# Relative-position stage by pairs of heads, with the first head's maxima inside it

## The reference

```python
qkv = x @ qkv_w + qkv_b                       # x: layer-normed, S = 2304 tokens, 12 heads of 32
attn = einsum('bqd,bkd->bqk', q * scale, k)
rel_h = einsum('bhwc,hkc->bhwk', qr, Rh)      # Rh[y, k] = rel_pos_h[y - k + 47]
rel_w = einsum('bhwc,wkc->bhwk', qr, Rw)
bias = (rel_h[..., :, None] + rel_w[..., None, :]).reshape(B * nh, S, S)
out = softmax(attn + bias) @ v
x = x + out @ proj_w + proj_b                 # then x + experts(layernorm(x)), two of eight by gates
```

## Time and profile before

| | us |
|---|---|
| median of 3 runs (lowest, highest) | 2328.25 (2328.11, 2330.27) |
| the profiled execution, its own time | 2332.33 |
| its span | 2330.6 |
| TensorE busy | 2061.9 (88%) |
| VectorE busy | 1783.8 (77%) |
| ScalarE busy | 1661.2 (71%) |
| GpSimd busy | 756.0 (32%) |

### The profile page before, as it was taken

How to read it: one execution, slowest core, us unless ns; L and a number is a source line. 1 busy time by engine, 2 the same in 40 slices (tenths; PEclk the granted TensorE clock), 3 DMA queues, 4 the chain that set the end, 5 groups by cost and what they waited for, 6 DMA issues and landing times. The chain is left out here.

```text
span 2330.6 us, 38125 instructions
## 1 busy us (share of the span) xinstructions
PE 2061.9 (88%) x12356; PEld 1882.0 (81%) x12356; DVE 1783.8 (77%) x3335; ACT 1661.2 (71%) x2909; POOL 756.0 (32%) x523
## 2 busy tenths in 40 slices
PE   6933347999999999999999999965799999999997
PEld 6922226888888888888888888744799999999997
DVE  5654446999999999999999998556677777777774
ACT  3344405888888888888888888912577778877785
POOL 0030031445444554445454445530122211221121
PEclk9955577999999999999999999977799999999999
DMA  6778893465544655546555454132566766777774
GB/s 208 223 164 188 189 168 72 85 127 101 105 95 77 125 106 101 103 76 116 107 101 113 78 106 79 57 122 93 170 212 215 223 216 215 220 219 226 214 211 115
DMA packets 123366, 334.59 MB, mean 144 GB/s; under 512 B 17648, under 2 KB 56008, under 8 KB 117860
## 3 DMA queue, kind: packets, MB, share of 16 engines
q1 hardware_dynamic: 111888, 312.42, 54.2%
q0 software_dynamic: 10400, 19.87, 3.9%
q10 hardware_dynamic: 960, 0.80, 0.1%
HBM read 269.62 MB, written 63.43 MB: 143 GB/s over the span
## 5 line engine op out<-in xcount | busy, mean ns | idle before, releaser
L891 DVE TENSOR_REDUCE mx<-ps_m 128x1 f32<-128x384 f32 x1212 | 643.4, 553 | 102.4 <-PE ps_m L746 96.8
L842 ACT ACTIVATE p_hi<-ps_s 128x768 fp32r<-128x768 f32 x648 | 528.2, 815 | 138.8 <-PE ps_s L760 135.3
L595 POOL TENSOR_TENSOR p_lo<-p_f,p_hi 128x768 fp32r<-128x768 f32 x216 | 398.8, 1846 | 614.9 <-ACT p_f L848 614.9
L848 ACT ACTIVATE p_f<-ps_s 128x768 f32<-128x768 f32 x648 | 525.1, 810 | 1.3 <-POOL p_lo L595 1.3
L746 PE MATMUL ps_m<-key_hi,query_hi 128*128 128x384 f32 x1240 | 418.2, 344 | 49.6 <-DMA query_hi<-rel_hi_d 40.2
L595 DVE TENSOR_TENSOR p_lo<-p_f,p_hi 128x768 fp32r<-128x768 f32 x432 | 417.0, 965 | 38.8 <-ACT p_f L848 37.9
L1580 ACT CAST w_hi<-w_raw 128x384 fp32r<-128x384 f32 x600 | 290.2, 516 | 135.8 <-PE ps_o L1557 130.3
L1698 DVE TENSOR_TENSOR w_lo<-w_raw,w_hi 128x384 fp32r<-128x384 f32 x600 | 316.5, 556 | 79.0 <-ACT w_hi L1580 78.9
L757 PE MATMUL ps_s<-query_hi,key_hi 128*128 128x384 f32 x1296 | 338.7, 342 | 12.5 <-DMA query_rest<-m_d 10.4
L770 PE MATMUL ps_o<-p_hi,val 128*65 128x384 f32 x1296 | 331.7, 337 | 1.8 <-POOL p_lo L595 1.6
L760 PE MATMUL ps_s<-query_rest,key_rest 121*128 121x384 f32 x1296 | 332.2, 338 | 0.0
(11 more groups left out here) (209 smaller groups left out, 2927.8 us busy)
## 6 DMA issues: line engine op xcount, KB each, us to landing
w_raw<-w_u SPq DMA_DIRECT2D x200, 576.0 KB, 4.6
query_rest<-rel_lo_d SPq DMA_DIRECT2D x36, 864.0 KB
query_rest<-qk_lo_d SPq DMA_DIRECT2D x36, 576.0 KB
query_rest<-qk_hi_d SPq DMA_DIRECT2D x36, 576.0 KB
rel_lo_d<-out_lo SPq DMA_DIRECT2D x6, 1728.0 KB, 30.6
query_hi<-rel_hi_d SPq DMA_DIRECT2D x12, 864.0 KB, 18.5
v_d<-v_sb SPq DMA_DIRECT2D x6, 1170.0 KB, 7.5
val<-v_d SPq DMA_DIRECT2D x12, 585.0 KB, 7.3
```

The lines of the kernel that those rows point to most:

```text
L595: engine.tensor_tensor(p_lo[r][:], p_f[idx % 2], p_hi[r][:].bitcast(F32), ALU.subtract).then_inc(lo_done(0, idx)[0], 1)
L842: act.activation(p_hi[r][:], ps_s[:, bank:bank + 2, 0:TB], ACT.Exp).then_inc(hi_ok, 1)
L848: act.activation(p_f[idx % 2], ps_s[:, bank:bank + 2, 0:TB], ACT.Exp).then_inc(f_ok, 1)
L891: dve.tensor_reduce(mx[s // TILES][:, s // 3 % 6, col:col + 1], ps_m[:, c, 0:TB], AX.X, ALU.max).then_inc(mx_ok, 1)
```

## The change

- `phase_qkv`: queries are stored apart from keys, to `q_d`, laid out per head as 32 high rows and 32 rest rows (`store_q`, six DMAs a block); keys by `store_k`; each block's queries of the first two heads are loaded back at once into `q0`. The relative table is loaded, padded with zeros and split here, on GpSimd. Buffers that were apart now share room with those of later phases (`w_raw` with `v_sb`, for one).
- `phase_rel`: six pairs of heads instead of three groups of four. The 128 partitions of the query operand hold high, rest, high, rest. The two tables' results stand on partitions 64 to 111 and 0 to 47 of one buffer, stored as 112 rows by two heads; two buffers for pairs. A fill has four values of c by 96 columns, 24 fills per pair. The first head's operands are loaded after the first pair's store, and its 42 chunks of maxima run between the fills from the third pair on, the last 12 behind the last fill. Both one-hot builds are here.
- `phase_attention`: starts with the first head's operands and maxima in place. `query_hi`'s relative rows are loaded from a padded layout (two halves of 64 rows, 48 of each used), query_rest's queries as one load of 64 rows.
- one identity matrix for all phases; `xt_hi` has room of its own.

```diff
@@ phase_qkv, SyncE @@
+            def store_q(blk, par):
+                sp.wait_ge(hi_ok, OPB * blk + KC)
+                sp.wait_ge(lo_ok, OPB * blk + KC)
+                for part, v in enumerate((qk_hi, qk_lo)):
+                    for m in range(KC):
+                        sp.dma_start(q_d[m * HPT:(m + 1) * HPT, part, :, blk * TB:(blk + 1) * TB],
+                                     v[par][:, m, :].bitcast(F32)).then_inc(q_out[par], 16)
+            def store_k(blk, par):
...
+                for v, d in ((qk_hi, k_hi_v), (qk_lo, k_lo_v)):
+                    sp.dma_start(d[:, :, blk * TB:(blk + 1) * TB], v[par][:, KC:QK_TILES, :].bitcast(F32)).then_inc(st_out[par], 16)
...
+            def load_q0(blk, par):
+                sp.wait_ge(q_out[par], Q_STORES * (blk // 2) + 2 * Q_STORES)
+                cols = slice(blk * TB, (blk + 1) * TB)
+                for h in range(RH):
+                    sp.dma_start(q0[:, h, cols].bitcast(F32),
+                                 q_d[h:h + 1, :, :, cols].rearrange("a r d n -> a (r d) n").broadcast_to([2, 2 * HD, TB])).then_inc(q0_in, 16)
+            for blk in range(BLOCKS):
+                par = blk % 2
+                store_q(blk, par)
+                store_k(blk, par)
...
+                if blk == BLOCKS - 1:
+                    load_q0(blk, par)
+                store_v(blk, par)
+                if blk < BLOCKS - 1:
+                    load_q0(blk, par)
@@ phase_qkv, ScalarE @@
                 act.wait_ge(st_out[par], 48 * i + 48)
+                act.wait_ge(q_out[par], Q_STORES * i + Q_STORES)
@@ phase_rel, SyncE @@
             def load_q(g):
...
+                for h in range(RH):
+                    sp.dma_start(q_sb[g % 2][:, h, :].bitcast(F32),
+                                 q_d[g * RH + h:g * RH + h + 1].rearrange("a r d n -> a (r d) n").broadcast_to([2, 2 * HD, S])).then_inc(q_in[g % 2], 16)
+            def store(g):
+                sp.wait_ge(r_hi, FILLS * (g + 1))
+                sp.wait_ge(r_lo, FILLS * (g + 1))
+                for o, d in ((out_hi, rel_hi_d), (out_lo, rel_lo_d)):
+                    sp.dma_start(d[g * RH:(g + 1) * RH, 0:BOTH, :].rearrange("h r n -> r h n"),
+                                 o[g % 2][0:BOTH, :, :].bitcast(F32)).then_inc(r_out[g % 2], 16)
...
+            load_q(1)
+            for g in range(GROUPS):
+                if g + 2 < GROUPS:
+                    sp.wait_ge(ps_ok, FILLS * (g + 1))
+                    load_q(g + 2)
+                store(g)
+                if g == 0:
+                    sp.wait_ge(hot_ok, HOT_STEPS // 2 - 1)
+                    load_keys(sp, 0, keys[0], k_hi_d, hi_in)
+                    sp.wait_ge(hot_ok, HOT_STEPS)
+                    load_rest_keys(sp, 0, keys[1], k_hi_d, k_lo_d, val, v_d, rest_in)
+                    sp.wait_ge(r_out[0], 32)
+                    load_query(sp, 0, query_hi, q_d, rel_hi_d, hi_in)
+                    load_query_rest(sp, 0, 0, query_rest, q_d, rel_lo_d, rest_in)
+                if g == GROUPS - 1:
+                    store_max(0)
+                    store_max(1)
...
@@ phase_rel, TensorE @@
+            for n in range(ALL):
...
+                for k in range(CPB):
+                    c = f % HALF * CPB + k
+                    if a == 0:
+                        out = ps[0:UP, bank, 0:TB].rearrange("r (c h y) -> r c h y", h=RH, c=CPB)[:, k, :, :]
+                        last = pe.matmul(out, tab[:, 0, UP + SIDE - 1 - c:2 * UP + SIDE - 1 - c], q_sb[g % 2][:, :, c:S:SIDE],
+                                         start=True, stop=True)
...
+                last.then_inc(ps_ok, 1)
+                for s in chunk_after.get(n, ()):
+                    chunk(s)
+            for s in range(CHUNKS - BEHIND, CHUNKS):
+                chunk(s)
@@ new helpers, called in phase_rel and phase_attention @@
+def load_query(sp, h, query_hi, q_d, rel_hi_d, ok):
+    sp.dma_start(query_hi[0:HD, :].bitcast(F32), q_d[h, 0, :, :]).then_inc(ok, 16)
+    sp.dma_start(query_hi[HD:P, :].bitcast(F32), rel_hi_d[h, :, :].rearrange("(a r) n -> a r n", a=2)[:, 0:SIDE, :]).then_inc(ok, 16)
+def load_query_rest(sp, h, b, dst, q_d, rel_lo_d, ok):
...
+    sp.dma_start(dst[0:2 * HD, :, :].bitcast(F32), shared(q_d[h, :, :, cols].rearrange("r d n -> (r d) n"))).then_inc(ok, 16)
```

More of the change, by code:

```diff
@@ L34, with phase_qkv @@
 LN2_EPS = 1e-5
-def phase_qkv(nc, x, qkv_w, qkv_b, qkv_b_t, qk_hi_d, qk_lo_d, v_d):
+def phase_qkv(nc, x, qkv_w, qkv_b, qkv_b_t, rel_t, q_d, k_hi_d, k_lo_d, v_d, ident, room, keys, query_hi, query_rest, q0, tab_raw, tab):
     GT = 6
@@ L331, with one_hots @@
 RING = 4
-def one_hots(pool, key_hi, key_rest, hot, done):
-    made = 0
+def one_hots(pool, key_hi, key_rest, hot, done, made=0):
     half = SIDE // 2
@@ L363, in one_hots, with phase_rel @@
             pool.wait_ge(done, made)
+    return made
 HOT_STEPS = 14
-def phase_rel(nc, rel_t, qk_hi_d, qk_lo_d, rel_hi_d, rel_lo_d, room, key_hi, key_rest):
+def phase_rel(nc, q_d, k_hi_d, k_lo_d, v_d, rel_hi_d, rel_lo_d, m_d, ident, q0, tab, room, keys, query_hi, query_rest, val, mx):
     with ExitStack() as ctx:
@@ L425, in group @@
[L425 to L436, removed]
@@ L456, in _ @@
+            one_hots(pool, keys[2], keys[3], hot[:], hot_ok, made)
         @block.tensor
         def _(pe):
-            pe.wait_ge(tab_ok, 1)
-            with pe.Fori(0, GROUPS) as g:
-                for f in range(FILLS):
-                    a, bank = ORDER[f // (FILLS // 2)], f % BANKS
-                    if a == 1 and f * CPB % (SIDE // Q_PARTS) == 0:
-                        pe.wait_ge(q_in[f * CPB // (SIDE // Q_PARTS)], 48 * g + 48)
-                    pe.wait_ge(r_lo, FILLS * g + f + 1)
-                    for n in range(CPB):
-                        c = (f * CPB + n) % SIDE
-                        own = slice(c, S, SIDE) if a == 0 else slice(c * SIDE, (c + 1) * SIDE)
-                        last = pe.matmul(ps[0:SIDE, bank, n * NQ:(n + 1) * NQ],
-                                         tab[:, a, SIDE - 1 - c:REL - c], q_sb[:, :, own], start=True, stop=True)
-                    last.then_inc(ps_ok, 1)
@@ new lines, in _ @@
+            for n in range(ALL):
+                g = n // FILLS
+                if n % FILLS == 0 and g >= 2:
+                    dve.wait_ge(r_out[g % 2], 32 * (g // 2))
+                dve.wait_ge(r_hi, n + 1)
+                dve.tensor_tensor(places(out_lo, n), results(n), places(out_hi, n).bitcast(F32), ALU.subtract).then_inc(r_lo, 1)
+                for s in chunk_after.get(n, ()):
+                    chunk(s)
+            for s in range(CHUNKS - BEHIND, CHUNKS):
+                chunk(s)
@@ L523, in phase_attention @@
+def phase_attention(nc, q_d, k_hi_d, k_lo_d, rel_hi_d, rel_lo_d, v_d, m_d, o_d, sums_d, ident, keys, query_hi0, query_rest0, val0, mx, room):
     with ExitStack() as ctx:
@@ L1120, in _, with phase_gates @@
                 measured(blk)
[L1123 removed]
+def phase_gates(nc, gate_w, gate_b, xn_d, ident, x1, stats, xt_hi, xt_lo, gate, rank):
     with ExitStack() as ctx:
```

425 lines of the change are left out of this document (221 added, 204 removed).

## The result

The changed kernel takes **2655.56 us** (median of 4 runs, 2653.85 to 2659.89) against 2329.26 for the kernel before (4 runs, 2328.11 to 2331.24): ratio 1.1403, 95% interval [1.1383, 1.1422]. The forecast was 2675. The profiled execution spans 2658.1 us; that of before 2330.6, so 327.5 are to be accounted for.

The account below looks back on a forecast made before the run. Transfers pace the 241 us between QKV and first scores; TensorE paces QKV and attention. 2330.6 + 167 (QKV and relative stage) + 180 (attention) = 2678 of span, forecast 2675; range 2480 to 2800.

Parts of the forecast that it names:

- The deciding quantity: All new transfers: over how many of 16 DMA engines each is spread, limited by the smaller outermost count, 4 or 2.
- two weak signs: Profile before: DMA share 0.64 and 0.42 ending attention batches with 8-row loads; no landing shown for a 12-row transfer.
- The second sign: View of issues: a landing for query_hi's 96 relative rows, none for rsum<-rec_d with 12 rows, so not on all 16.
- QKV: Busiest engine needs 28 us a block against 15.8; next stage starts at 197 instead of 125.4, +72.
- The relative stage: Between QKV and first scores: 305 of transfers, 24 of fills, 7 of turn, 336 us; +167 with QKV's 72.
- Costs order, not time: Relative stage: SP's wait for the first pair's store delays later issues but keeps the ring full; no time priced.
- Attention: Late query_hi stalls 11 us in heads 2 to 11 (110), 15 in head 1, plus 55 of slower clock: +180.
- The loss of clock: Attention: after each of 11 stalls, TensorE runs some 11 us at 8 products for 14, losing 5 each: 55 us.
- The rest: Rest of the kernel: identity matrix built once and xt_hi in its own room, 0 us.
- Rival A': Attention: transfers narrow but hidden in the heads, so only +167 remains: 2495 us; chance 0.08.
- Rival C: Only part of the limit binds (SBUF side's count, or narrow transfers rotating over engines): about 2245 us; chance 0.07.
- Rival B: Transfers spread over all 16 engines, VectorE sets the relative stage, first scores at 259: 2221 us; chance 0.15.

Follow-up runs that it names:

- the best kernel: Changed kernel with all three transfers cut, queries laid out by channel, load halves alternating and head 1's operands issued earlier: 2256.24 us, ratio 0.9686 to the kernel before.

## Why the prediction was right

**The deciding quantity** was rightly named, and the inference from two weak signs in the profile of before held: shares of 0.26 and 0.13 at counts 4 and 2, and the waits come and go with the count alone (129.9, 40.7 and 13.9 us at 2, 4 and 8). The second sign, a missing landing in the view of issues, is weaker than the prediction took it: in the profile after, query_hi<-rel_hi_d has lost its landing, but so has query_hi<-q_d, a load of 32 rows on the same semaphore, and both have one again where the relative half alone is cut in two. It marks the semaphore, not the transfer. The Trainium skill's rule, that a transfer runs on the largest number up to 16 that divides both outermost counts ("DMA: Bandwidth & Descriptors", section "Why a DMA increments its semaphore by 16 and not by 1"), agrees with all of these. Here the other side's count (128, 96) was always a multiple of the small one, so no run here tells this rule from "the smaller count".

**QKV.** 28 us a block, and the next stage at 197: it started at 193.9, which is 27.4 a block by the same formula. Right in size and cause: with the query stores alone cut, the issue of the next pair comes at 167 instead of 194.

**The relative stage.** 336 us and first scores at 533: 341.7, and 535.6. The term that carries it, five pair loads of 43.5 us, follows from the rate of one engine, and 54 GB/s over two engines is that rate. "Costs order, not time" held for SyncE's early wait. One thing in it was not foreseen: SyncE doesn't only wait, it is also held inside the issue itself (below), while the DMA share stays at 0.13 (220 to 240).

**Attention.** Waits 125 forecast, 129.9 measured: 11 for each common head (10.8), but 15 for head 1, which took 22.3, since its operands queue behind two more batches. The loss of clock was over-priced: 55 against 30.3 (160.2 less 129.9). I had taken that the low clock lasts 11 us behind a wait, from the earlier trace rows, where TensorE had come out of the long half-idle stage; behind a wait of 10 us it lasts 6 (693.76 to about 700), which by the same working (8 products for 14) is 2.7 us lost each. So attention is +160 and not +180. This term alone is 25 us too large, more than the whole error of the forecast (2675 against 2656); the waits (5 too small) and the stage with QKV (2.5 too small) took some of it back.

**The rest**, forecast at 0, is -2.2. The edits priced at nothing showed no cost with everything spread either: with the layout by channel the stage starts at 126.1, against 125.4 before the change.

**The rivals.** Rival A', narrow but hidden in the heads, falls by the 11 waits. Rival C falls too: the SBUF side's count stayed at 96 while the waits went from 129.9 to 13.9, and loads of count 2 that follow each other never share more than two engines (0.13 from 220 to 240, 280 to 300 and 380 to 400). Rival B was wrong in its condition and also in its price: with everything spread, the kernels take 2288 and 2266, and not 2221. Of the 2266, its own terms were: QKV right (stage at 126), the stage 160 instead of 132 (I had VectorE set its length; the loads' half rate leaves the DMA engines to set it), and attention +12 for head 1's late operands, which I had at 0. The stage's term was read from the wrong row: 433 GB/s was measured on 128 partitions. The row beside it, stores from 48 partitions at 196 with the engines 0.98 busy, already showed that full engines can move half as much, and a load in two halves is nearer to that.

## What to carry to other kernels

Before a transfer is merged into one instruction, read the outermost count on both sides after the rearrangement: a 2 or a 4 in front (halves, copies, heads) ran on 2 or 4 of 16 DMA engines here, in all three transfers, and what stood behind it in the queue came late too (the stores of rel_hi_d landed 37.6 us after their issue, with all three cut 15.7). In a profile the sign is a DMA share that stands at 0.13 or 0.26 while an engine waits for a DMA; such a low share was a full queue. The cure here was a memory layout that puts the long dimension outermost, not many small issues: 24 issues a block for the same bytes moved QKV's limit from the engines to SyncE (19.7 us a block where 15.8 are needed), and the layout gave it back.

## What the runs showed that was not expected

- Issuing a DMA took SyncE 20 to 40 us where narrow transfers were queued ahead. Its issues in the stage of the changed kernel:

```profile
208.75 27.15 SPq L480 DMA_DIRECT2D q<-q_d  x2
...
241.54 21.45 SPq L487 DMA_DIRECT2D rel_lo_d<-out_lo  x1
...
369.94 39.94 SPq L487 DMA_DIRECT2D rel_hi_d<-room  x1
```

  In the kernel with the new layout most of these stores' issues take 0.3 to 0.8 us (at 230.69: 0.37), though the DMA engines are full there too (share 0.95 from 225 to 230, 1.02 from 230 to 235). So it isn't a full share that holds SyncE; that it is the length of the two narrow engines' queues fits, but no run here shows it.
- Transfers of 32 to 64 rows of 9216 bytes move 196 to 234 GB/s with all DMA engines full, loads and stores alike; stores from 112 partitions and a load to 128 move 409 to 435. Alternating halves gave 8 to 9% at most. What sets it is open. It fits the best kernel's stage of 160 us too, in which the DMA share is 0.87.
- Cutting a transfer of outermost count 2 into two of 64 rows gave a factor of about 4 (54 against some 220 GB/s), not 8.
- A wait of some 2.6 us costs TensorE nearly as much again in clock (23 us behind ten such waits and one of 14.6), and a wait of 11 little more (28 behind eleven; both against the kernel with query_hi cut, each less its waits).
- The maxima one pair later took away a wait of 19.9 us and left one of 22.6 on another name. Where the DMA engines are full, the name on a wait says little about what would remove it.
